# Turning the normalised rows of three batches on VectorE, by way of DRAM, two heads later

## What is computed

```python
def _layernorm(x, axis=-1, eps=1e-05):
    m = jnp.mean(x, axis=axis, keepdims=True)
    v = jnp.var(x, axis=axis, keepdims=True)
    return (x - m) / jnp.sqrt(v + eps)
...
    qkv = (x @ w_qkv).reshape(b, n, 3, H, DH).transpose(2, 0, 3, 1, 4)
    q, k, v = (qkv[0], qkv[1], qkv[2])
    q = q * SCALE
    sim = jnp.einsum('bhid,bhjd->bhij', q, k)
    sim = jnp.tanh(sim / SOFTCAP) * SOFTCAP
...
    out = jnp.einsum('bhij,bhjd->bhid', attn, v)
    gates = jax.nn.sigmoid(x @ w_gates)
...
    x = x + _L0_attn_ref(_layernorm(x, axis=-1), L0_attn_w_qkv, L0_attn_w_gates, L0_attn_w_out)
    x = x + _L0_xattn_ref(_layernorm(x, axis=-1), itok_BxS_13_99985, ctx_2048, ctx_2048, ctx_2048)
    x = x + _L0_ffn_ref(_layernorm(x, axis=-1), ...)
```

## Time and profile before

| | us |
|---|---|
| median of 3 runs | 1596.42 (1595.49 to 1596.97) |
| the profiled execution | 1598.12 |
| its span, first to last instruction | 1596.4 |
| PE busy in it | 1563.7 (98%) |
| DVE busy in it | 1030.9 (65%) |

### The profile page before, as it was taken

The page is one execution under the profiler, slowest core; times in us unless marked ns, Lnnn a source line. Parts: engine busy times, 40 slices in busy tenths (PEclk is TensorE's granted clock), DMA queues, the critical chain, the costliest instruction groups (busy, mean ns, idle before and its releaser), DMA issues.

```text
span 1596.4 us, 24261 instructions
## 1 busy us (share of the span) xinstructions
PE 1563.7 (98%) x8012; PEld 1352.6 (85%) x8013; DVE 1030.9 (65%) x2219; ACT 584.1 (37%) x997; POOL 448.0 (28%) x378
## 2 busy tenths in 40 slices
PE   7999999999999999999999999999999999999996
PEld 5888888888888888888888887788999989999995
DVE  4798767788777788777787778655663582222221
ACT  4454443434434334434334334333111312333332
POOL 3445332234123234222233221102200003333342
PEclk9999999999999999999999999999999999999998
DMA  8886564677676786776686776564621026778753
GB/s 290 282 305 211 184 219 146 237 279 260 256 268 226 261 303 238 257 282 224 243 312 248 297 303 241 165 209 157 239 94 54 7 105 211 235 201 267 211 87 40
DMA packets 97601, 345.37 MB, mean 216 GB/s; under 512 B 10144, under 2 KB 24992, under 8 KB 92000
## 3 DMA queue, kind: packets, MB, share of 16 engines
q1 hardware_dynamic: 84480, 306.33, 52.7%
q0 software_dynamic: 13024, 37.79, 10.1%
HBM read 224.03 MB, written 120.05 MB: 216 GB/s over the span
## 4 chain that ended last, share of the span: by engine, by line
PE 90%; DVE 5%; DMA 2%; POOL 1%; issue 1%; ACT 1%; SPq 0%; POOLq 0%; DVEq 0%; ACTq 0%
PE bank L360 29%; PE bank L362 28%; PE bank L361 28%; PE bank L1912 1%; PE bank L2029 1%; DMA wqk_raw<-wqk_in 1%; DMA wqk<-wqk_parts 1%; POOL store L633 0%; DVE resid L1235 0%; PE bank L1702 0%; DMA wv_raw<-wv_in 0%; DMA rows<-x_rows,ids_e 0%; POOL wqk L633 0%; PE bank L1986 0%; DVE place_hot L1591 0%
## 5 line engine op out<-in xcount | busy, mean ns | idle before, releaser
L674 POOL TENSOR_TENSOR probs<-probs,causal 128x256 f32<-128x256 f32 x126 | 90.5, 739 | 412.5 <-ACT probs L852 412.5
L360 PE MATMUL bank<-store,wqk 128*128 128x512 f32 x512 | 201.8, 394 | 0.3 <-DMA wqk<-wqk_parts 0.3
L362 PE MATMUL bank<-store,wqk 128*128 128x512 f32 x512 | 202.1, 395 | 0.0
L361 PE MATMUL bank<-store,wqk 128*128 128x512 f32 x512 | 201.8, 394 | 0.0
L1235 DVE SCALAR_TENSOR_TENSOR resid<-bank,factor,resid 128x512 f32<-128x512 f32 x256 | 189.4, 741 | 1.2 <-PE bank L362 1.1
L633 POOL TENSOR_TENSOR pre_split<-pre_raw,pre_split 128x1528 fp32r<-128x1528 f32 x34 | 120.6, 3548 | 140.9 <-ACT pre_split L814 140.9
L850 ACT ACTIVATE probs<-bank 128x512 f32<-128x512 f32 x189 | 85.8, 528 | 131.1 <-PE bank L362 131.1
L362 PEld LDWEIGHTS bank<-store,wqk 128*128 128x128 f32 x512 | 96.0, 188 | 22.9
L1229 DVE TENSOR_TENSOR q_lo<-bank,q_hi 128x512 fp32r<-128x512 f32 x64 | 44.3, 692 | 108.2 <-ACT q_hi L897 108.1
L361 PEld LDWEIGHTS bank<-store,wqk 128*128 128x128 f32 x512 | 96.0, 188 | 20.8
L360 PEld LDWEIGHTS bank<-store,wqk 128*128 128x128 f32 x512 | 96.0, 188 | 20.5 <-DMA wqk<-wqk_parts 0.8
(11 more groups left out here) (333 smaller groups left out, 3927.1 us busy)
## 6 DMA issues: line engine op xcount, KB each, us to landing
pre_parts<-pre_split SPq DMA_DIRECT2D x34, 1528.0 KB, 6.7
wqk<-wqk_parts SPq DMA_DIRECT2D x96, 512.0 KB, 4.6
pre_raw<-pre SPq DMA_DIRECT2D x34, 764.0 KB, 7.7
store<-wv_parts SPq DMA_DIRECT2D x12, 2048.0 KB, 9.0
wo<-wo_parts SPq DMA_DIRECT2D x48, 512.0 KB, 8.8
expert_w<-pre_parts SPq DMA_DIRECT2D x8, 2816.0 KB, 11.9
wqk_parts<-wqk SPq DMA_DIRECT2D x16, 1024.0 KB, 5.0
expert_w<-pre_parts SPq DMA_DIRECT2D x8, 1536.0 KB, 8.9
```

The lines of the kernel that those rows point to most:

```text
L360: nc.tensor.matmul(out_ap, a_hi, b_hi, start=first, stop=False)
L361: nc.tensor.matmul(out_ap, a_hi, b_lo, start=False, stop=False)
L362: return nc.tensor.matmul(out_ap, a_lo, b_hi, start=False, stop=last)
L674: nc.gpsimd.tensor_tensor(diagonal, diagonal, causal[:, :, :], ALU.mult).then_inc(S["masked"], 1)
```

## The change

The 12 tiles of batches 2 to 4 are no longer turned by PE. SP stores each tile of `xn` to a new DRAM tensor `xn_rows` (heads h = 8 and 9, two tiles each), loads it back with `load_turned` into the same place (h = 9 and 10, two tiles and so eight DMAs each), and DVE turns it with one block transpose into bank 2. This and the hi and lo parts come in heads h = 10 to 13 now, in place of 8 to 11, and the gates in h = 14, in place of 12. As block turns give the columns in another order (column 4 m + k in chunk k), the rows of the weights of q, k, v and the gates are laid out so on the host, and PE's transposes of the first batch read every fourth column. `v_product` waits only for its own tile.

```diff
@@ -323,6 +325,7 @@
         LN_X, LN_IN = 2, 5
+        XN_TURN = LN_IN + 5
...
-            t = h - LN_IN - 3
+            t = h - XN_TURN
...
-            return b + 1 if b + 1 < BATCH and h == LN_IN + 3 + TB else None
+            return b + 1 if b + 1 < BATCH and h == XN_TURN + TB else None
...
+            def store_xn(t):
+                sp.wait_ge(S["xn_ready"], t + 1)
+                sp.dma_start(xn_rows[t * P:(t + 1) * P], xn[:, t % TB, :]).then_inc(S[f"xn_stored{t % TB}"], 16)
+
+            def turn_xn(t):
+                sp.wait_ge(S[f"xn_stored{t % TB}"], 16 * (t // TB))
+                load_turned(xn[:, t % TB, :], xn_rows[t * P:(t + 1) * P], S[f"xn_turned{t % TB}"])
...
+                b, h = divmod(u, HEADS)
+                if b + 1 < BATCH and LN_IN + 3 <= h < LN_IN + 6:
+                    half = TB // 2
+                    first = TB * (b + 1) + half * (h - LN_IN - 4)
+                    if h > LN_IN + 3:
+                        for t in range(first, first + half):
+                            turn_xn(t)
+                    if h < LN_IN + 5:
+                        for t in range(first + half, first + 2 * half):
+                            store_xn(t)
...
+            def turn_xn(t, to, u):
+                dve.wait_ge(S["tanh_done"], 3 * u)
+                dve.wait_ge(S[f"xn_turned{t % TB}"], 16 * QUADS * (t // TB))
+                turn(xn[:, t % TB, :], bank[to]).then_inc(S["xnT_ready"], 1)
...
                 lo_part(k_lo[:, :], bank[1][:, :], k_hi[:, :], "qk_hi_done", "k_lo_done", 2 * u + 2)
+                if xnT_slot(u) is not None:
+                    turn_xn(xnT_slot(u), 2, u)
                 if u >= 2:
                     y_add(u - 2, 1)
...
-                    last = nc.tensor.transpose(bank[to][:, k * P:k * P + P], xn[:, t % TB, k * P:k * P + P], ident[:, :])
+                    last = nc.tensor.transpose(bank[to][:, k * P:k * P + P], every(xn[:, t % TB, :], k), ident[:, :])
...
-                if t is not None:
-                    pe.wait_ge(S["tanh_done"], 3 * u)
-                    transpose_xn(t, 2)
...
-                    pe.wait_ge(S["xnT_lo_done"], TB * (n // TB // GROUPS) + TB)
+                    pe.wait_ge(S["xnT_lo_done"], TB * (n // TB // GROUPS) + n % TB + 1)
```

More of the change, by code:

```diff
@@ L246, in build @@
         pre_parts = nc.dram_tensor("pre_parts", (P, 2, PRE_COLS), F32, kind="Internal").ap()
+        xn_rows = nc.dram_tensor("xn_rows", (T, D), F32, kind="Internal").ap()
         xs = nc.dram_tensor("xs", (XTILES * P, D), F32, kind="Internal").ap()
@@ L260, in build @@
         ct_loaded sh_loaded
-        scat0 scat1 scat2 scat3 gath0 gath1 gath2 gath3 gath4 gath5 gath6 gath7 x_added table_ready ids_ready x3_stored0 x3_stored1 x3_turned0 x3_turned1 e_added sh_zeroed
+        scat0 scat1 scat2 scat3 gath0 gath1 gath2 gath3 gath4 gath5 gath6 gath7 x_added table_ready ids_ready xn_stored0 xn_stored1 xn_stored2 xn_stored3 xn_turned0 xn_turned1 xn_turned2 xn_turned3 x3_stored0 x3_stored1 x3_turned0 x3_turned1 e_added sh_zeroed
         logits_read minus_max exp_router
@@ L1086, in ln_apply, with turn @@
                                         ALU.subtract, ALU.mult).then_inc(S[done], 1)
+            def turn(tile, to=bank[XT]):
+                return nc.vector.transpose(to[:, :], tile.rearrange("p (a y k) -> p k a y", a=QUADS, y=BLOCK))
             def count(w, prefix, prefix_done):
@@ L1411, in xT_low @@
                 nc.vector.tensor_tensor(xT_lo[:, :, :], bank[XT][:, :].rearrange("p (k n) -> p k n", k=KC), xT_hi[:, :, :].bitcast(F32), ALU.subtract).then_inc(S[f"{ph}_xT_lo"], 1)
-            def turn(tile):
-                return nc.vector.transpose(bank[XT][:, :], tile.rearrange("p (a y k) -> p k a y", a=QUADS, y=BLOCK))
             def turn_rows_x(i, j):
@@ L2107 @@
         "token_ids": c(f(itok_BxS_13_99985).reshape(TILES, P).T),
-        "wqk_in": c(f(L0_attn_w_qkv)[:, :2 * HEADS * DH].reshape(KC, P, 2, HEADS, DH).transpose(3, 1, 2, 0, 4)),
-        "wv_in": c(f(L0_attn_w_qkv)[:, 2 * HEADS * DH:].reshape(KC, P, GROUPS, TB * DH).transpose(2, 1, 0, 3)),
-        "wgates": c(wg.reshape(KC, P, P).transpose(1, 0, 2)),
+        "wqk_in": c(f(L0_attn_w_qkv)[:, :2 * HEADS * DH].reshape(P, KC, 2, HEADS, DH).transpose(3, 0, 2, 1, 4)),
+        "wv_in": c(f(L0_attn_w_qkv)[:, 2 * HEADS * DH:].reshape(P, KC, GROUPS, TB * DH).transpose(2, 0, 1, 3)),
+        "wgates": c(wg.reshape(P, KC, P)),
         "wo_in": c(f(L0_attn_w_out).reshape(HEADS, DH, D)),
```

## The result

The changed kernel takes 1600.64 us in the median of 8 runs (1599.98 to 1603.38), the kernel before 1596.52 in 8 runs beside it: 4.1 us slower, ratio 1.0029 with a 95% interval of 1.0018 to 1.0040. The forecast was 1600.7 and slower. The profiled execution took 1600.53 us, with a span of 1598.8 and a granted clock of 0.997, as before.

What follows compares the result with a forecast made beforehand. PE, busy 98% and 90% of the chain, was taken to bound the kernel. 12 x (0.83 - 0.42) = +4.9 us, less 0.64 for head 13, gave +4.3 on 1596.42: 1600.7 us, range 1597.0 to 1606.0.

Steps and rivals of the forecast that it cites:

- the first: Rival: in turning heads PE's transpose time comes back and `y_add` 2 is still in time; 1590.7 us, faster; 8%.
- PE's 0.42 a tile: Four transposes a tile removed from PE in the attention: 12 tiles by 0.42, 5.0 us, all on the path.
- The second rival: In turning heads the new wait is about as long as the transposes were; 1596 to 1599 us, not measurable; 20%.
- DVE's chain, start to start: Turning head, K the start of `k_hi`: the turn adds 1.00 us; `y_add` 2 ends at K + 6.47, wanted at K + 5.75.
- The price of the wait: PE waiting for bank 7 before output tile 3: turning head 0.64 + 0.19 = 0.83 us longer than a plain one.
- Head 13's 0.64 taken off once: Head 13's old wait, from a late `wqk_raw`, goes because the gates no longer stand ahead of it: 0.64 us less.
- The gates: Moved from h = 12 to 14, their head keeps its work: zero, bounds minus 0.2 and plus 0.2 us.
- SP: Added issues, about 0.45 us each, 3.7 for eight, ending ahead of the q weights in head 26; cost zero.
- The sum: Whole kernel: 12 x (0.83 - 0.42) = +4.9, less 0.64, makes +4.3 us; median 1600.7 us.
- two chains: Turning heads of batch 1: ACT's `v_high` ends near K + 5.1, tying with DVE's K + 5.13; priced at nothing, up to 0.1.

Runs made afterwards that it cites:

- experiments 6: Changed kernel with DVE's turn in two halves of 256 columns, one ahead of `q_lo`, one at the old place; 1598.14 us, ratio 1.0010 to the kernel before.
- 4: Changed kernel with DVE's turn done twice at its place; 1612.61 us in one execution.
- experiment 1: Changed kernel with DVE's turn moved to the start of the head, ahead of `q_lo`; 1594.98 us, ratio 0.9990 to the kernel before.
- experiment 7: Changed kernel with the turn ahead of `q_lo` and every turn one head later (h = 11 to 14); 1592.65 us, ratio 0.9971 to the kernel before.
- 5: Changed kernel with `sum_keys` behind `y_add` 2 in the twelve turning heads; 1594.60 us, ratio 0.9988 to the kernel before.
- experiments 2: Kernel before with the turns two heads later and `v_product` waiting for its own tile; PE turns, no DMAs; 1597.03 us, ratio 0.9999.
- 3: Kernel before with the later place plus SP's stores and loads of the tiles, PE still turning; 1596.77 us, ratio 0.9999.
- 8: Kernel before with only the host's new weight row order and PE's strided reads; 1597.11 us, ratio 1.0000.

## Why the prediction was right, and where its steps were off

**The mechanism is shown.** DVE's turn pushes `y_add` 2 past the moment at which PE wants bank 7. The dose series (experiments 6, the changed kernel, 4) gives a head longer by just what PE is late; taking the turn out of that chain without taking it away (1, 7) or taking something else out (5) removes the wait; the place and the DMAs without it (2, 3) cost nothing. Of the rivals, the first (PE's 0.42 a tile comes back and no wait takes its place) is false for the changed kernel and true of experiment 7, where 12 x 0.42 = 5.0 us come back. That the rival's sum and the gain of that attention are both 5.7 is chance: the rival took head 13's 0.64 off, which experiment 7 still pays (15.60), and the rest there is head 61's 0.61, which nobody foresaw. The second rival (a wait of 0.42 to 0.7 a head) came close: the wait is 0.76, midway between its upper end and my 0.83, and the attention's +2.8 stands at its upper end of +2.7; only the medians, 1600.6 and 1600.7, are clearly outside its 1596 to 1599.

**DVE's chain, start to start.** K + 0.67, 2.27, 4.53, 5.13, 5.73 were forecast for `k_lo`, `y_add` 1, `xnT_low`, `v_low`, `y_add` 2; the trace has 0.67, 2.29, 4.52, 5.11, 5.71. The end was forecast at 6.47 and is 6.43.

**The price of the wait: 0.83 forecast, 0.76 measured.** This term was mis-sized. I took it from head 13 as a whole (0.64 over plain, plus 0.19). The direct difference was there in the same rows: PE's load at K + 6.33 against K + 5.75 is 0.58, and 0.58 + 0.19 is 0.77. The remaining 0.06 of head 13 is no part of this wait; where it comes from I don't know.

**Head 13's 0.64 taken off once** is right for the changed kernel, as that head is now one of the twelve at 15.67. The reason given for it, that the gates no longer stand ahead of it, is wrong: in experiments 2 and 3 the wait for `wqk_raw` is there at head 13 (1.07 us on ACT); in the changed kernel the wait for DVE hides it, and in experiments 1 and 7, where DVE is out of the way, head 13 has 15.51 and 15.60 again.

**The gates** moved at +0.03 a head, inside the bounds of 0.2.

**SP** was priced at 0.45 us a load and 3.7 for eight. The median load is 0.44, but some take up to 1.28, and the eight of head 26 took 5.82, and the weights behind them start later than forecast:

```profile
427.81 0.61 SPq L445 DMA_DIRECT2D pre_raw<-pre  x1
428.47 5.82 SPq L375 DMA_DIRECT2D rows<-xn_rows  x8
434.33 0.43 SPq L442 DMA_DIRECT2D wo<-wo_parts  x1
434.81 0.43 SPq L438 DMA_DIRECT2D wqk<-wqk_parts  x1
```

The q weights left SP a microsecond after the `q_hi` of their head, in place of with it. Nobody waited for them, so the sum is right here by its slack and not by its working.

**Head 61, not foreseen: 0.6 us less.** In the kernels that turn on PE (before, 2, 3, 8) PE waits 0.77 us there for the q weights, the head takes 12.77 to 12.79; in the six that turn on DVE it is 12.17 or 12.18. The trace has the load that PE waits for: the q weights that SP issues with the `q_hi` of head 61 land 9.6 us after that in the kernel before and in 3, and 8.2 us in the changed kernel and in 7, where PE wants them after 8.9. Neither the layout alone (8) nor the DMAs (3) or the place (2) brings the shorter times. Why the turn on DVE does is open.

**The sum.** Forecast +4.3 us; the heads of the two profiles give +2.8 and +3.1, the medians +4.1 and +3.8. With 0.76 in place of 0.83 and head 61 the working gives 12 x (0.76 - 0.42) - 0.64 - 0.60 = +2.8, which is what the attention has. The last microsecond of the medians is thus not explained by the steps, and the hit to the tenth is partly luck. The spans of the two profiles differ by 2.4 only: that of before was taken in an execution 1.6 above its median, that of the changed kernel in one 0.1 below. The other kernels that turn on DVE show the same, the medians gaining less than the attention: 7 gained 5.7 in the attention and 4.3 in the medians, 1 gained 3.0 and 1.9, 5 gained 3.1 and 2.1. I can't settle where it lies.

One place outside the attention does vary. The part behind it has 635.2 to 639.6 us in the profiles of this study, yet from the `q_hi` of head 62 to PE's last matmul it is 621.5 to 622.5 in all of them. What differs is what follows, from that matmul's start to the end: 13.8 us in the changed kernel and 13.7 in before, but 15.9 in experiment 7, 15.8 in 2 and 18.1 in 1. There POOL adds the last tiles of the result to `out`, 39 indirect DMAs that each wait for the one before to land. The last ones of experiment 1, whose last matmul starts at 1578.07:

```profile
1575.74 1.55 POOL L790 DMA_INDIRECT out<-x_early,ids_e  x1 [3.94 <-DMA out<-x_early,ids_e]
1581.28 1.55 POOL L790 DMA_INDIRECT out<-x_early,ids_e  x1 [4.00 <-DMA out<-x_early,ids_e]
1586.68 1.55 POOL L790 DMA_INDIRECT out<-x_early,ids_e  x1 [3.85 <-DMA out<-x_early,ids_e]
```

One every 5.5 us: when this queue has fallen behind, two of them are still to come after PE's end, and the kernel ends by it. That explains the spread of single profiles, and not the two main ones, which are alike there.

**Busy shares.** That PE is the engine with the highest share did not make its relief a gain: 12 x 0.42 us went from PE and 12 x 0.76 came back as waits. The Trainium skill, "Perfetto Trace Analysis", section "Identifying the Most-Contended Engine", taken alone, missed that. The same page of the Trainium skill, in its section "Optimization Strategies" for DMAs, says to optimize the engines on the critical path that the idle matmul engine waits for, and experiments 1, 5 and 7 agree. The Trainium skill's preference for TensorE in "VectorE: DVE Perf Modes", section "Rules for kernel authors", agrees with the changed kernel (0.42 on PE against 0.76) and not with experiment 7: what decided was the place in DVE's order, not the engine.

## What to carry to other kernels

Before moving work from the bound engine to one that is 65% busy, find the result of that engine which the bound one waits for next, and count the slack to it, start to start; work ahead of that result costs one for one once the slack is gone, however idle the engine is elsewhere. Then look in the same engine's order for the gap where it waits itself, and put the work there, with its input a whole period early. Where two chains come out equally long on paper, both have to be shortened before anything is gained.

## What the runs showed of the hardware

A 64 KB load of 512-byte pieces took 2.0 us to land in the x stage and 5.3 us in the median among the attention's weights. The rows of the changed kernel (DMA issues, us to landing):

```profile
xn_rows<-rows SPq DMA_DIRECT2D x12, 256.0 KB, 5.8
rows<-xn_rows SPq DMA_DIRECT2D x48, 64.0 KB, 5.3
```

SP's issue of such a load took 0.44 us in the median among the attention's transfers (0.32 to 1.28) and 0.32 in the x stage; eight together took 5.82 us in head 26, and 4.62 in head 9 of experiment 1. Four PE transposes that read every fourth column take 0.03 us more than four that read 128 columns in a row.
